# A four-layer graph network: TensorE's outputs and the residual rows by tile in the first node stage, and the combining first in the first node layer

## The chip, the cores and the metric

The kernel runs on one core of one Trainium2 chip. The time is the device time of one execution in microseconds (us), and the median of several runs is compared. Before the change it is 8783.5 us (3 runs, 8773.5 to 8791.46).

## What is computed

50,000 nodes with 160 features each (64 scalars and 32 vectors of three parts) pass four graph layers. Each layer gathers and weighs messages along 50,000 edges sorted by their target, sums them by node, combines the sums with the node's own row, adds the row of before and normalises. The two places that the change touches are the node half of layer 0 and the node half of layer 1:

```python
# layer 0, the node half; a0 = node_attr
x = node_input + _merge(ps, pv)
s2, v2 = _eq_ln(x, ln2_w0, ln2_b0, ln2_w1)
fs, fv = _eq_lin(s2, v2, f1_ws, f1_bs, f1_wv)
fs = fs * a0
fv = fv * a0[:, :, None]
sc = silu(fs[:, :M0])
fv = fv * sigmoid(fs[:, M0:])[:, :, None]
os_, ov = _eq_lin(sc, fv, f2_ws, f2_bs, f2_wv)   # 64 scalars, 32 vectors
os_ = os_ * a0
ov = ov * a0[:, :, None]
return x + _merge(os_, ov)
# around every layer
x = _layernorm(x + layer(x, ...), axis=-1)
# layer 1, the node half
return sc + alpha * conv
```

All is float32.

## The kernel before

A chunk is 512 nodes: 4 tiles (TILES) of 128, one node to a partition. There are 98 chunks. The work is a row of stages, and each stage goes over all chunks before the next begins: set-up, `node_pre`, `edge_logits`, `edge_softmax`, a join, `node_first` (the first node stage, layer 0), then for layers 1 to 3 `edge_layer`, a join and `node_layer`.

In a stage every engine has its own program, written out in order by `pipeline(engine, chunks, stages)`: in round i each listed step runs for chunk i minus its offset, in the order of the list. Four rounds are the body of a hardware loop; the first and last rounds are written out. The engines meet by semaphores alone: a step waits until a counter shows that another engine's step for some chunk is done. So the order on one engine is fixed, and a step that waits holds up all behind it.

`node_first`, in the order of one round i:

- TensorE (PE): `turn_last` (i-5, transposes of the normalised rows), `turn_norm` (i-2, transposes of `scaled`), `outputs` (i-3), `hidden` (i-2), `turn_sums` (i), `mix_last` (i-5, the rows for the next layer's gather), `project` (i).
- ScalarE (ACT): `copy_out` (i-5), `final_norm` (i-4), `copy_norm` (i-2), `gates` (i-2), `copy_sums` (i), `rows_out` (i-5).
- VectorE (DVE): `activate` (i-3), `final_bias` (i-4), `scale` (i-2), `residual` (i-1), `divide` (i), `combine` (i-3).
- GpSimd (POOL): gathers of the summed messages (i), and the two roots.
- SyncE (SP): loads and stores.

`project`, `outputs` and `mix_last` write the same PSUM columns (two banks from column 1024 on). In `outputs` the bias comes first as one product of the identity with 256 columns, then four products of 64 columns add the scalars on it, then six of 64 columns write the vectors; PSUM holds the 256 scalars of the 4 tiles, then the 384 vector columns by part. VectorE's `combine` takes, for each tile, one operation for the scalars and one for the vectors, multiplies by the node's attribute and adds `base`, which `residual` has written in the same order (L1832). `final_sums` ends with a copy of 8 columns, the row's tail (L712).

`node_layer(1)`, in the order of one round i: VectorE `before` (i; here one operation on 128x4, L884, which needs the gathered sums), `final_bias` (i-2), `combine` (i-1). GpSimd: four gathers for chunk i (L671), then the root of chunk i-2 (L720). TensorE: `front` (i), `turn_out` (i-3), `back` (i), `mix_out` (i-3). ScalarE: `front`, `copy_out` (i-3), `final_norm` (i-2), `rows_out` (i-3). SyncE loads the indices and rows of chunk i once `before` of chunk i-2 is done. Layer 2 has the same lists with a longer `before`; layer 3 has `combine` first.

Of the kernel before, what the change touches and what calls it, by code (L numbers as in the profile page):

```python
# [22 lines left out]
ALU = mybir.AluOpType  # L23
# [3 lines left out]
P = 128  # L27
CHUNK = 512
TILES = CHUNK // P
C0, C1 = 64, 32  # L30
# [121 lines left out]
def gnn_kernel(nc, inp, out):  # L152
# [9 lines left out]
    def two(name, shape, dt=F32, own=None):  # L162
        return [sb(f"{name}_{k}", shape, dt, own) for k in range(2)]
# [16 lines left out]
    with ctx:  # L180
# [589 lines left out]
        def node_layer(layer):  # L770
# [13 lines left out]
            with nc.Block() as block:  # L784
# [88 lines left out]
                def _(dve):  # L873
# [97 lines left out]

                    if with_e:
                        pipeline(dve, chunks, [(before, 0), (lambda s: final_bias(dve, s), 2), (combine, 1)])
                    else:
                        pipeline(dve, chunks, [(combine, 1), (lambda s: final_bias(dve, s), 2), (before, 0)])
# [664 lines left out]
        def node_first():  # L1640
            den_steps, x1_steps, scale_steps, hidden_steps = 10, 2 * TILES + 8, 7, 1
            sum_steps = 2 * TILES + 2 * TILES + 2
            m_at, q_at, v_at, r_at, c_at, b_at, n_at = 48, 56, 60, 68, 76, 84, 88
            SCA, VEC, HID_S, HID_V, GATE = 1024, 1024 + XS, 2048, 2560, 3584
            with ExitStack() as own, nc.Block() as block:
                shares, scaled = two("shares", [P, XD], own=own), two("scaled", [P, XD], own=own)
                squares, base = two("squares_1", [P, XD - XS], own=own), [sb(f"base_{k}", [P, XW], own=own) for k in range(4)]
                first = two("first", [P, XD], own=own)
# [15 lines left out]
                def _(pe):  # L1664
# [20 lines left out]
                    def project(s):  # L1685
                        read = sum_step.after((s.g - 2) * sum_steps - (sum_steps - 2 * TILES))
                        precompute(pe, ets_sb.after(s.g - 4), read)
# [13 lines left out]
                    def mix_last(s):  # L1701
                        read = sum_step.after(ahead(s.g, 3, chunks) * sum_steps - (sum_steps - 2 * TILES))
# [26 lines left out]
                    def outputs(s):  # L1729
                        read = mid_step.after(ahead(s.g, 3, chunks) * x1_steps - (x1_steps - 2))  # L1730
                        precompute(pe, read, ets_sb.after(s.g - 2))
                        pe.wait_ge(ready.sem, 1)
                        pe.wait_ge(ets_sb.sem, ets_sb.after(s.g - 2))
                        pe.wait_ge(gate_sb.sem, gate_sb.after(s.g + 1))
                        pe.wait_ge(hidden_step.sem, hidden_step.after((s.g + 1) * hidden_steps))
                        pe.wait_ge(mid_step.sem, read)
                        pe.matmul(flat[:, SCA:SCA + XS], ident, W("f2_b"), start=True, stop=False)
                        for t in range(TILES):
                            pe.matmul(flat[:, SCA + t * C0:SCA + (t + 1) * C0], hid_s[:, t * P:(t + 1) * P], W("f2_s"),
                                      start=False, stop=(t == TILES - 1))  # L1740
                        for i in range(3):
                            for k in range(2):
                                to = flat[:, VEC + i * P:VEC + (i + 1) * P].rearrange("p (h k c) -> p h k c", h=2, k=2)
                                last = pe.matmul(to[:, :, k, :], hid_v[:, (2 * i + k) * P:(2 * i + k + 1) * P], W("f2_v"),
                                                 start=True, stop=True)
                        last.then_inc(post_mm.sem, 1)
# [4 lines left out]
                @block.scalar  # L1751
                def _(act):
                    def copy_norm(s):
                        act.wait_ge(xt2_mm.sem, xt2_mm.after(s.g + 1))
# [8 lines left out]
                    def gates(s):  # L1763
# [6 lines left out]
                    pipeline(act, chunks, [  # L1770
                        (lambda s: copy_out(act, s, TURN), 5), (lambda s: final_norm(act, s), 4), (copy_norm, 2),
                        (gates, 2), (copy_sums, 0), (lambda s: rows_out(act, s, SCA), 5)])

                @block.gpsimd
                def _(pool):
                    pipeline(pool, chunks, [
                        (lambda s: gather_sums(pool, s, 0, mid_step, x1_steps), 0),
                        (lambda s: root(pool, s, v_at, 2 * TILES, mid_step, x1_steps, root_sb), 2),
                        (lambda s: root(pool, s, 32, TILES, sum_step, sum_steps, root2_sb, 1), 4)])

                @block.vector
                def _(dve):
# [30 lines left out]
                    def residual(s):  # L1813
# [5 lines left out]
                        dve.wait_ge(sum_step.sem, sum_step.after((s.g - 2) * sum_steps))  # L1819
                        dve.wait_ge(scale_step.sem, scale_step.after((s.g - 1) * scale_steps))  # L1820
                        dve.wait_ge(pre_step.sem, pre_step.after((s.g + 1) * den_steps))
                        k = chain.did(dve.tensor_tensor(x1[:, 0:XS], flat[:, SCA:SCA + XS], x[:, 0:XS], ALU.add).then_inc(chain.sem, 1))
                        k = chain.did(dve.tensor_tensor(x1[:, XS:], flat[:, VEC:VEC + XD - XS], x[:, XS:XD], ALU.add).then_inc(chain.sem, 1))
                        chain.did(dve.tensor_copy(b[:, XD:], x[:, XD:]).then_inc(chain.sem, 1))
                        dve.wait_ge(chain.sem, chain.after(k))
# [5 lines left out]
                            ALU.add).then_inc(chain.sem, 1))  # L1831
                        chain.did(dve.tensor_tensor(b[:, 0:XD], x1[:], x[:, 0:XD], ALU.add).then_inc(chain.sem, 1))  # L1832
                        dve.wait_ge(chain.sem, chain.after(c))
# [6 lines left out]
                    def scale(s):  # L1840

                        chain = Chain(scale_step, s.g, scale_steps)
                        dve.wait_ge(chain.sem, chain.after(0))
                        st, x1, to, attrs = stats[s.quad], first[s.slot], scaled[s.slot], base[s.quad][:, XD:XD + TILES]
                        dve.wait_ge(root_sb.sem, root_sb.after(s.g + 1))
# [30 lines left out]
                    def combine(s):  # L1876
# [367 lines left out]
```

## Time and profile before

| | |
|---|---|
| median of 3 runs | 8783.5 us |
| profiled execution | 8718.24 us, span 8716.4 us |
| TensorE busy | 6567.3 us (75%) |
| VectorE busy | 6227.6 us (71%) |
| ScalarE, GpSimd busy | 4108.6 us (47%), 5093.1 us (58%) |
| granted TensorE clock, mean | 0.853 |
| `node_first` | from about 2600 to 3980 us of the span |
| node half of layer 1 | from about 4785 to 5480 us of the span |

The shares are means over ten stages with different limits. What counts for the change is which wait ends last within one round of the two stages. The clock is given as a part of 2.4 GHz; its lower level is 0.5.

### The profile page before, as it was taken

How to read it: one execution, taken by the hardware profiler on the slowest of the kernel's cores; microseconds unless marked ns; L12 is line 12 of the kernel's file. 1: busy time of each engine (PE TensorE's matmuls, PEld its weight loads, DVE VectorE, ACT ScalarE, POOL GpSimd, SP SyncE). 2: the span in 40 equal slices, each digit the busy share in tenths (PEclk: the TensorE clock that was granted, in tenths of full speed). 3: DMA queues.
4: the chain of work that ended last, by engine and by line, in shares of the span. 5: the costliest groups of instructions: out<-in, count | busy, mean ns of one | idle time of the engine just before them, and what ended most of it. 6: DMA issues, size and time to landing. Idle time of an engine off the chain costs nothing. (4 is left out here: it accounts for less than half of the span.)

```text
span 8716.4 us, 182003 instructions
## 1 busy us (share of the span) xinstructions
PE 6567.3 (75%) x41992; PEld 5838.5 (67%) x41992; DVE 6227.6 (71%) x20668; ACT 4108.6 (47%) x9608; POOL 5093.1 (58%) x4620
## 2 busy tenths in 40 slices
PE   3667777774557888888998666899865679999555
PEld 3455666664447777777888666788755569998554
DVE  4667888885548888885665667566588877775787
ACT  1334555552224444444444667444366654444444
POOL 4668888884435444444554777555466644443777
PEclk9887888885559999999999888899978889999665
DMA  6872333337873333333444566445455544443555
GB/s 133 182 173 79 89 89 88 90 85 145 164 155 92 99 96 99 99 98 102 125 126 114 181 190 192 120 123 125 110 169 166 170 129 120 119 120 106 154 162 155
DMA packets 910393, 1118.45 MB, mean 128 GB/s; under 512 B 458518, under 2 KB 546422, under 8 KB 910032
## 3 DMA queue, kind: packets, MB, share of 16 engines
q1 hardware_dynamic: 728032, 812.69, 33.4%
q0 software_dynamic: 182144, 303.64, 14.7%
q14 instruction: 175, 1.43, 0.1%
q8 instruction: 42, 0.69, 0.0%
HBM read 650.35 MB, written 465.65 MB: 128 GB/s over the span
## 5 line engine op out<-in xcount | busy, mean ns | idle before, releaser
L451 POOL DMA_INDIRECT erow<-e_rows,edge_idx x1176 | 1247.3, 1061 | 1229.6 <-issue 1137.3
L671 POOL DMA_INDIRECT agg<-seg_rows,edge_idx x1568 | 1554.3, 991 | 656.4 <-issue 483.2
L720 POOL TENSOR_TENSOR stats<-stats,power 128x8 f32<-128x8 f32 (+1 forms) x588 | 751.8, 1279 | 866.1 <-DVE xo L712 444.4
L400 PE MATMUL banks<-w_all,xt 128*128 128x128 f32 (+1 forms) x2352 | 546.2, 369 | 795.7 <-DVE y_more L945 259.5
L400 PEld LDWEIGHTS banks<-w_all,xt 128*128 128x128 f32 x2352 | 429.3, 248 | 879.8 <-issue 872.2
L486 PEld LDWEIGHTS banks<-seg,mid 128*128 128x128 f32 x7840 | 931.9, 194 | 15.1
L486 PE MATMUL banks<-seg,mid 128*128 128x128 f32 x7840 | 933.4, 277 | 0.0
L534 ACT ACTIVATE mid_t<-banks 128x512 f32<-128x512 f32 x980 | 585.1, 597 | 315.3 <-PE banks L486 311.7
L403 PE MATMUL banks<-w_all,xt 128*128 128x128 f32 x3528 | 657.7, 339 | 0.0
L403 PEld LDWEIGHTS banks<-w_all,xt 128*128 128x128 f32 x3528 | 617.5, 254 | 0.0
L498 PE MATMUL banks<-w_all,mid_t 128*128 128x161 f32 (+1 forms) x2352 | 583.9, 330 | 2.8 <-ACT res L539 2.8
L539 ACT ACTIVATE res<-banks 128x644 f32<-128x644 f32 (+1 forms) x294 | 218.0, 742 | 687.4 <-PE banks L505 685.5
L1207 POOL DMA_INDIRECT work<-src_table,edge_idx x392 | 456.0, 1163 | 108.2 <-issue 108.2
L608 POOL DMA_INDIRECT row_of_dram<-where_back x196 | 255.4, 1303 | 363.1 <-DMA where_back<-place_dram 315.8
L1207 POOL DMA_INDIRECT y<-dst_table,edge_idx x392 | 387.5, 989 | 119.5 <-issue 119.2
L474 PE MATMUL banks<-w_all,hid_p 128*128 128x384 f32 (+1 forms) x1176 | 454.8, 509 | 3.2 <-ACT hid_p L516 3.2
L738 ACT ACTIVATE xo<-y,stats 128x64 f32<-128x64 f32 (+1 forms) x1200 | 428.8, 443 | 45.7 <-DVE stats L727 45.7
L498 PEld LDWEIGHTS banks<-w_all,mid_t 128*128 128x128 f32 x2352 | 378.9, 192 | 89.2 <-issue 38.4
L738 ACT ACTIVATE xo<-y_more,stats 128x64 f32<-128x64 f32 (+1 forms) x1152 | 411.4, 443 | 38.6 <-DVE stats L727 38.5
L505 PE MATMUL banks<-w_all,mid_t 128*128 128x64 f32 x2352 | 423.7, 262 | 0.0
L500 PE MATMUL banks<-w_all,mid_t 128*128 128x96 f32 x2352 | 421.2, 260 | 0.0
L337 DVE TENSOR_TENSOR seg<-dst_row,edge_idx 128x512 f32<-128x512 int32 x294 | 203.1, 691 | 281.9 <-PE banks L486 244.4
(276 smaller groups left out, 18225.2 us busy)
## 6 DMA issues: line engine op xcount, KB each, us to landing
x_rows<-xo SPq DMA_DIRECT2D x294, 324.0 KB, 2.6
xin<-x_rows SPq DMA_DIRECT2D x294, 324.0 KB
e_rows<-ets SPq DMA_DIRECT2D x294, 322.0 KB
dst_row<-in_dst_flat SPq DMA_DIRECT2D x294, 256.0 KB
xin<-in_x SPq DMA_DIRECT2D x196, 324.0 KB, 7.1
seg_rows<-res SPq DMA_DIRECT2D x196, 322.0 KB, 2.6
seg_rows<-res SPq DMA_DIRECT2D x98, 384.0 KB, 2.3
seg_rows<-res SPq DMA_DIRECT2D x98, 338.0 KB, 6.6
```

What stands on the lines that cost most here:

```text
L400: pe.matmul(flat[:, to + k * cols:to + (k + 1) * cols], of[:, k * P:(k + 1) * P], W(w_s), start=True, stop=True)
L403: last = pe.matmul(flat[:, to + 2 * cols + k * P:to + 2 * cols + (k + 1) * P], of[:, (2 + k) * P:(3 + k) * P], W(w_v), start=True, stop=True)
L451: pool.indirect_dma_start(erow[s.quad][:, t, 0:EROW], None, table, bass.IndirectOffsetOnAxis(idx[s.slot][:, t:t + 1], 0),).then_inc(rows_i ...
L474: last = pe.matmul(psum[:, 2 + k, 0:2 * w_cols], hid_p[:, k * P:(k + 1) * P], W(f"fc2_{layer}"), start=True, stop=True)
L486: last = pe.matmul(psum[:, SEG[k], t * P:(t + 1) * P], mid[s.slot][:, t, k * P:(k + 1) * P], seg[s.slot][:, t, :], start=True, stop=True)
L498: pe.matmul(post[:, t, 0:v_at + 96], mid_t[s.slot][:, 0, cut], W(f"pa{layer}"), start=True, stop=False)
L505: last = pe.matmul(post[:, t, v_at + 32:v_at + 96], mid_t[s.slot][:, 2, cut], W(f"pc{layer}"), start=False, stop=True)
L534: act.activation(mid_t[s.slot][:, k, :], bank(SEG[k]), ACT.Copy).then_inc(agg_sb.sem, 1)
L671: pool.indirect_dma_start(agg[s.quad][:, t, 0:SUM_COLS[layer]], None, seg_rows[layer], bass.IndirectOffsetOnAxis(idx[s.slot][:, t:t + 1], ...
L720: pool.tensor_tensor(st[:, at + n:at + 2 * n], st[:, at:at + n], power[:, 0:n], ALU.pow) \
L738: last = act.activation(to, of if at == 0 else of.rearrange("p (i c) -> p i c", i=3), ACT.Identity, bias=st[:, 40 + t:41 + t], scale=st[:, ...
L1207: pool.indirect_dma_start(to[s.slot][:, t, :], None, table, bass.IndirectOffsetOnAxis(idx[s.slot][:, first + t:first + t + 1], 0),).then_i ...
```

## The change

In `node_first`:

- `outputs` writes one run of 160 columns for each tile (64 scalars, then the vectors), two tiles to a PSUM bank. The bias is no longer one product of 256 columns but one of 64 columns for each tile, right ahead of the product that adds on it. 14 products to a chunk where there were 11 (each is two weight loads and two matmuls in the trace).
- `residual` writes `base` in rows of 160 columns for each tile: one operation for the scalars, one for the vectors, instead of one for all; it has one more wait, for a normalisation three chunks back, since ScalarE now reads `base`.
- `combine` has one operation of 160 columns for each tile instead of two.
- The tail of the row is copied by ScalarE, ahead of `final_norm`.

In `node_layer(1)` VectorE runs `combine` (i-1), `final_bias` (i-2), `before` (i).

```diff
-                    if with_e:
+                    if layer == 2:
                         pipeline(dve, chunks, [(before, 0), (lambda s: final_bias(dve, s), 2), (combine, 1)])
                     else:
                         pipeline(dve, chunks, [(combine, 1), (lambda s: final_bias(dve, s), 2), (before, 0)])
...
+            row_at = (0, 512, D, 512 + D)
...
-                        pe.matmul(flat[:, SCA:SCA + XS], ident, W("f2_b"), start=True, stop=False)
                         for t in range(TILES):
-                            pe.matmul(flat[:, SCA + t * C0:SCA + (t + 1) * C0], hid_s[:, t * P:(t + 1) * P], W("f2_s"),
-                                      start=False, stop=(t == TILES - 1))
+                            to = flat[:, SCA + row_at[t]:SCA + row_at[t] + C0]
+                            pe.matmul(to, ident, W("f2_b", cols=(0, C0)), start=True, stop=False)
+                            pe.matmul(to, hid_s[:, t * P:(t + 1) * P], W("f2_s"), start=False, stop=True)
...
+                    def norm(s):
+                        act.wait_ge(sum_step.sem, sum_step.after((s.g + 1) * sum_steps))
+                        act.wait_ge(node_out[s.quad].sem, node_out[s.quad].after(s.quarter))
+                        act.activation(xo[s.quad][:, XD:], base[s.quad][:, TILES * D:], ACT.Copy)
+                        final_norm(act, s)
...
+                        dve.wait_ge(norm_sb.sem, norm_sb.after(s.g - 3))
...
-                        chain.did(dve.tensor_tensor(b[:, 0:XD], x1[:], x[:, 0:XD], ALU.add).then_inc(chain.sem, 1))
+                        rows = by_tile(b[:, 0:TILES * D])
+                        chain.did(dve.tensor_tensor(rows[:, :, 0:C0], by_tile(x1[:, 0:XS]), by_tile(x[:, 0:XS]), ALU.add).then_inc(chain.sem, 1))
+                        chain.did(dve.tensor_tensor(rows[:, :, C0:].rearrange("p t (i c) -> p i t c", i=3), by_part(x1[:, XS:]),
+                                                    by_part(x[:, XS:XD]), ALU.add).then_inc(chain.sem, 1))
...
-                            a = b[:, XD + t:XD + t + 1]
-                            chain.did(dve.scalar_tensor_tensor(
-                                yy[:, t, 0:C0], by_tile(flat[:, SCA:SCA + XS])[:, t, :], a, by_tile(b[:, 0:XS])[:, t, :],
+                            a = b[:, TILES * D + t:TILES * D + t + 1]
+                            k = chain.did(dve.scalar_tensor_tensor(
+                                yy[:, t, :], flat[:, SCA + row_at[t]:SCA + row_at[t] + D], a, b[:, t * D:(t + 1) * D],
                                 ALU.mult, ALU.add).then_inc(chain.sem, 1))
-                            k = chain.did(dve.scalar_tensor_tensor(
-                                yy[:, t, C0:].rearrange("p (i c) -> p i c", i=3), by_part(flat[:, VEC:VEC + 3 * P])[:, :, t, :],
-                                a, by_part(b[:, XS:XD])[:, :, t, :], ALU.mult, ALU.add).then_inc(chain.sem, 1))
                         dve.wait_ge(chain.sem, chain.after(k))
-                        final_sums(dve, s, chain, b[:, XD:])
+                        final_sums(dve, s, chain, None)
```

TensorE in the body of `node_first`'s loop, before, from `project` over `turn_norm` and `outputs` to `hidden` (`banks` is PSUM, `w_all` the weights with the identity, `hid_s` and `hid_v` the hidden rows):

```order
466 L1692 MATMUL banks<-w_all 128x256
467 L1694 MATMUL banks<-w_all,xt 128x128 x2
468 L1697 MATMUL banks<-w_all,xt 128x128 x3
469 L394 MATMUL banks<-w_all,scaled 128x128 x5
470 L1737 MATMUL banks<-w_all 128x256
471 L1739 MATMUL banks<-w_all,hid_s 128x64 x4
472 L1744 MATMUL banks<-w_all,hid_v 128x2x32 x6
473 L1715 MATMUL banks<-xt,w_all 128x128 x4
```

The same place now:

```order
474 L1698 MATMUL banks<-w_all,xt 128x128 x3
475 L394 MATMUL banks<-w_all,scaled 128x128 x5
476 L1740 MATMUL banks<-w_all 128x64
477 L1741 MATMUL banks<-w_all,hid_s 128x64
478 L1740 MATMUL banks<-w_all 128x64
479 L1741 MATMUL banks<-w_all,hid_s 128x64
480 L1740 MATMUL banks<-w_all 128x64
481 L1741 MATMUL banks<-w_all,hid_s 128x64
482 L1740 MATMUL banks<-w_all 128x64
483 L1741 MATMUL banks<-w_all,hid_s 128x64
484 L1746 MATMUL banks<-w_all,hid_v 128x2x32 x6
485 L1716 MATMUL banks<-xt,w_all 128x128 x4
```

One wide product and four narrow ones have become eight narrow ones; nothing else moved on TensorE.

VectorE in the node half of layer 1, one round before (`agg` holds the gathered sums, `y` and `y_more` the rows of this chunk and the next):

```order
1668 L884 TENSOR_TENSOR stats<-agg,xin 128x4
1669 L726 REGISTER_ALU
1670 L727 SCALAR_TENSOR_TENSOR stats<-stats 128x4
1671 L930 REGISTER_ALU
1672 L932 REGISTER_ALU
1673 L943 TENSOR_TENSOR y<-banks,xin 128x4x64
1674 L945 TENSOR_TENSOR y<-banks,xin 128x3x4x32
```

And now, the end of one round and the head of the next:

```order
1645 L708 TENSOR_SCALAR stats<-stats 128x4
1646 L710 ISA
1647 L712 COPY xo<-xin 128x8
1648 L726 REGISTER_ALU
1649 L727 SCALAR_TENSOR_TENSOR stats<-stats 128x4
1650 L884 TENSOR_TENSOR stats<-agg,xin 128x4
1651 L138 REGISTER_ALU
1652 L138 COMPARE_AND_BRANCH
1653 L943 TENSOR_TENSOR y_more<-banks,xin 128x4x64
```

L884, which waits for gathered rows, stood ahead of the combining of the chunk before it (L943 to L712) and now stands behind it.

## Rows read from the trace of the kernel before

**Rows 1.** Busy time by stretch: `node_first`'s loop; columns in the first line.
```profile
core 0: us, PE busy (x) PEld busy (x) DVE busy (x) ACT busy (x) POOL busy (x), PEclk, DMA share, GB/s
2709.40:3909.00 1199.60, 997.45 (x7570) 947.54 (x7569) 1007.96 (x4620) 554.46 (x1392) 582.16 (x523) 0.94 0.33 98
```
**Rows 2.** Waits in `node_first` (2700 to 3900 us); columns in the first line.
```profile
engine line waited for: us in total, times, longest us
DVE hid_v L1871 <- issue: 68.0, 22, 3.3
...
PE banks L394 <- ACT xt L759: 57.5, 65, 0.9
PE banks L394 <- DVE scaled L1861: 45.9, 22, 2.3
```
**Rows 3.** Timeline of TensorE: each round's start of `project`; columns in the first line.
```profile
start us, us, engine line op out<-in xcount [idle before <-releaser]
3300.49 0.67 PE L1692 MATMUL banks<-w_all 128*128 128x256 f32 x2 [1.04 <-ACT ets L766]
3313.12 0.67 PE L1692 MATMUL banks<-w_all 128*128 128x256 f32 x2 [1.13 <-ACT ets L766]
3330.55 0.67 PE L1692 MATMUL banks<-w_all 128*128 128x256 f32 x2 [1.14 <-ACT ets L766]
...
3425.11 0.67 PE L1692 MATMUL banks<-w_all 128*128 128x256 f32 x2 [1.13 <-ACT ets L766]
3439.11 0.67 PE L1692 MATMUL banks<-w_all 128*128 128x256 f32 x2 [1.14 <-ACT ets L766]
```
**Rows 4.** Timeline of VectorE over the end of a loop body in `node_first`.
```profile
3302.66 0.42 DVE L1822 TENSOR_TENSOR first<-banks,xin 128x256 f32<-128x256 f32 x1 [0.44 <-PE banks L1697]
...
3311.53 0.17 DVE L712 COPY xo<-base 128x8 f32<-128x8 f32 x1
3314.88 0.95 DVE L1871 SCALAR_TENSOR_TENSOR hid_v<-tanh_g,banks 128x768 f32<-128x768 f32 x1 [3.18 <-issue]
...
3317.10 0.42 DVE L1861 TENSOR_TENSOR scaled<-scaled,stats 128x256 f32<-128x256 f32 x1
```
**Rows 5.** Timeline: TensorE's weight loads (PEld) and matmuls, one ScalarE row, `outputs` to `hidden`.
```profile
3304.17 0.30 PEld L1737 LDWEIGHTS banks<-w_all 128*128 128x128 f32 x2
3305.49 1.42 PEld L1744 LDWEIGHTS banks<-w_all,hid_v 128*128 128x128 f32 x12
3306.21 0.68 ACT L1756 ACTIVATE xt<-banks 128x640 f32<-128x640 f32 x1
3309.17 0.97 PEld L1725 LDWEIGHTS banks<-xt,w_all 128*128 128x128 f32 x8
3309.28 1.06 PE L1725 MATMUL banks<-xt,w_all 128*128 128x128 f32 x8
```
**Rows 6.** Timeline of VectorE in `node_first`: base rows, a 384-column operation, `combine`.
```profile
3305.47 0.81 DVE L1832 TENSOR_TENSOR base<-first,xin 128x640 f32<-128x640 f32 x1
3308.25 0.27 DVE L1884 SCALAR_TENSOR_TENSOR y<-banks,base 128x64 f32<-128x64 f32 x1
3310.03 1.01 DVE L692 BATCH_NORM_STATS2 stats<-y 128x6 f32<-128x160 f32 x4
...
3316.63 0.55 DVE L1858 TENSOR_TENSOR scaled<-first,stats 128x384 f32<-128x384 f32 x1
```
**Rows 7.** Timeline of VectorE in the node half of layer 1, one round.
```profile
5106.90 0.16 DVE L884 TENSOR_TENSOR stats<-agg,xin 128x4 f32<-128x4 f32 x1 [1.56 <-DMA agg<-seg_rows,edge_idx]
5109.02 1.27 DVE L953 SCALAR_TENSOR_TENSOR y<-agg,stats,y 128x160 f32<-128x160 f32 x4
5110.34 1.00 DVE L692 BATCH_NORM_STATS2 stats<-y 128x6 f32<-128x160 f32 x4
...
5111.84 0.17 DVE L712 COPY xo<-xin 128x8 f32<-128x8 f32 x1
```
**Rows 8.** Groups by line, layer 1's node half, 4900 to 5400 us.
```profile
line engine op names shapes xcount | busy us, mean ns | idle before us <-releasers
L671 POOL DMA_INDIRECT agg<-seg_rows,edge_idx x285 | 286.0, 1003 | 85.5 <-issue 85.2 <-DVE xo L712 0.3
L720 POOL TENSOR_TENSOR stats<-stats,power 128x4 f32<-128x4 f32 x72 | 74.7, 1038 | 54.6 <-DVE xo L712 52.9 <-DMA edge_idx<-row_of_dram 1.3
L884 DVE TENSOR_TENSOR stats<-agg,xin 128x4 f32<-128x4 f32 x72 | 11.9, 165 | 131.6 <-DMA agg<-seg_rows,edge_idx 130.3 <-DVE xo L712 1.3
```
**Rows 9.** The instructions of line L884: count, durations, first and last start.
```profile
L884 DVE TENSOR_TENSOR stats<-agg,xin x98: 161/164/225, 4792.8 to 5467.7; 128x4 f32<-128x4 f32 x98
```

More of the change, by code:

```diff
@@ L1640, in node_first @@
         def node_first():
-            den_steps, x1_steps, scale_steps, hidden_steps = 10, 2 * TILES + 8, 7, 1
-            sum_steps = 2 * TILES + 2 * TILES + 2
+            den_steps, x1_steps, scale_steps, hidden_steps = 10, 2 * TILES + 9, 7, 1
+            sum_steps = TILES + 2 * TILES + 1
+            row_at = (0, 512, D, 512 + D)
             m_at, q_at, v_at, r_at, c_at, b_at, n_at = 48, 56, 60, 68, 76, 84, 88
@@ L1646, in node_first @@
                 shares, scaled = two("shares", [P, XD], own=own), two("scaled", [P, XD], own=own)
-                squares, base = two("squares_1", [P, XD - XS], own=own), [sb(f"base_{k}", [P, XW], own=own) for k in range(4)]
+                squares, base = two("squares_1", [P, XD - XS], own=own), [sb(f"base_{k}", [P, TILES * D + 2 * TILES], own=own) for k in range(4)]
                 first = two("first", [P, XD], own=own)
@@ L1685, in project @@
                     def project(s):
-                        read = sum_step.after((s.g - 2) * sum_steps - (sum_steps - 2 * TILES))
+                        read = sum_step.after((s.g - 2) * sum_steps - (sum_steps - TILES))
                         precompute(pe, ets_sb.after(s.g - 4), read)
@@ L1701, in mix_last @@
                     def mix_last(s):
-                        read = sum_step.after(ahead(s.g, 3, chunks) * sum_steps - (sum_steps - 2 * TILES))
+                        read = sum_step.after(ahead(s.g, 3, chunks) * sum_steps - (sum_steps - TILES))
                         precompute(pe, read)
@@ L1736, in outputs @@
                         pe.wait_ge(mid_step.sem, read)
-                        pe.matmul(flat[:, SCA:SCA + XS], ident, W("f2_b"), start=True, stop=False)
                         for t in range(TILES):
-                            pe.matmul(flat[:, SCA + t * C0:SCA + (t + 1) * C0], hid_s[:, t * P:(t + 1) * P], W("f2_s"),
-                                      start=False, stop=(t == TILES - 1))
+                            to = flat[:, SCA + row_at[t]:SCA + row_at[t] + C0]
+                            pe.matmul(to, ident, W("f2_b", cols=(0, C0)), start=True, stop=False)
+                            pe.matmul(to, hid_s[:, t * P:(t + 1) * P], W("f2_s"), start=False, stop=True)
                         for i in range(3):
                             for k in range(2):
-                                to = flat[:, VEC + i * P:VEC + (i + 1) * P].rearrange("p (h k c) -> p h k c", h=2, k=2)
-                                last = pe.matmul(to[:, :, k, :], hid_v[:, (2 * i + k) * P:(2 * i + k + 1) * P], W("f2_v"),
+                                at, step = SCA + row_at[k] + C0 + i * C1, row_at[2 + k] - row_at[k]
+                                to = flat[:, at:at + 2 * step].rearrange("p (h c) -> p h c", h=2)[:, :, 0:C1]
+                                last = pe.matmul(to, hid_v[:, (2 * i + k) * P:(2 * i + k + 1) * P], W("f2_v"),
                                                  start=True, stop=True)
@@ L1770, in _ @@
                     pipeline(act, chunks, [
-                        (lambda s: copy_out(act, s, TURN), 5), (lambda s: final_norm(act, s), 4), (copy_norm, 2),
+                        (lambda s: copy_out(act, s, TURN), 5), (norm, 4), (copy_norm, 2),
                         (gates, 2), (copy_sums, 0), (lambda s: rows_out(act, s, SCA), 5)])
@@ L1778, in _ @@
                         (lambda s: root(pool, s, v_at, 2 * TILES, mid_step, x1_steps, root_sb), 2),
-                        (lambda s: root(pool, s, 32, TILES, sum_step, sum_steps, root2_sb, 1), 4)])
+                        (lambda s: root(pool, s, 32, TILES, sum_step, sum_steps, root2_sb), 4)])
                 @block.vector
@@ L1823, in residual @@
                         k = chain.did(dve.tensor_tensor(x1[:, XS:], flat[:, VEC:VEC + XD - XS], x[:, XS:XD], ALU.add).then_inc(chain.sem, 1))
-                        chain.did(dve.tensor_copy(b[:, XD:], x[:, XD:]).then_inc(chain.sem, 1))
+                        chain.did(dve.tensor_copy(b[:, TILES * D:], x[:, XD:]).then_inc(chain.sem, 1))
                         dve.wait_ge(chain.sem, chain.after(k))
@@ L1843, in scale @@
                         dve.wait_ge(chain.sem, chain.after(0))
-                        st, x1, to, attrs = stats[s.quad], first[s.slot], scaled[s.slot], base[s.quad][:, XD:XD + TILES]
+                        st, x1, to, attrs = stats[s.quad], first[s.slot], scaled[s.slot], base[s.quad][:, TILES * D:TILES * D + TILES]
                         dve.wait_ge(root_sb.sem, root_sb.after(s.g + 1))
```

## The prediction, made before the result was known

> **What bounds the kernel now.** I read the busy time by stretch first, to see which stages the change touches, then the waits of each of the two stages, then one round of each in the timeline. The sums are made against the profiled execution, 8718.24 us (span 8716.4); the median of the runs is 8783.5 us, 65 us or 0.75% more. I take the change in microseconds over unscaled, since 1% of it is about 1 us.
>
> In `node_first` TensorE and VectorE are each busy 83 to 84% of 1199.6 us [rows 1]. There are 87 rounds in 1200 us (65 and 22 waits before the transposes of `scaled`, L394, [rows 2]), so 13.79 us a round. The timeline shows that this mean is of two kinds [rows 3]. An ordinary round is 12.63 us (3300.49 to 3313.12). There TensorE decides: it stands still only for ScalarE's copies (1.13 us before `project`, and 57.5 / 65 = 0.88 us before the transposes of `scaled` [rows 2]), and VectorE waits for it (0.44 us before L1822 [rows 4]). Every fourth round is 14.0 us (3425.11 to 3439.11) or 17.43 us (3313.12 to 3330.55). At that place the loop's body ends on VectorE, and L1871 comes 3.18 us after the instruction before it, with "issue" as the reason [rows 4]; 22 such stalls add to 68.0 us, and TensorE's transposes of `scaled` then wait 45.9 us in 22 times, 2.09 us each, for VectorE's L1861 [rows 2]. The rest of the long rounds is the clock: its mean is 0.94 over 1199.6 us [rows 1]. With levels 1 and 0.5 it was at the lower one for 12%, 144 us, in which a busy TensorE loses half, 72 us. The sum closes: four rounds at 13.79 are 55.2, four at 12.63 are 50.5, so 4.7 us a loop, 22 loops, 103 us; 22 times 1.4 us (14.0 less 12.6) is 31, and 72 the clock.
>
> In the node half of layer 1 the round is (5467.7 - 4792.8) / 97 = 6.96 us [rows 9]. GpSimd waits for L712, the end of VectorE's combining, 52.9 us in 72 rounds, and VectorE's L884 waits for gathered rows, 130.3 us [rows 8]. Each waits for the other. From L884 at 5106.90 to the end of L712 at 5112.01 are 5.1 us [rows 7]; the root is 1.04, four gathers with their gaps (286.0 + 85.5) / 285 x 4 = 5.2 [rows 8]; what remains of two rounds (13.9) is some 2.5 us until the rows have landed. It is a ring of 13.9 us that spans two rounds.
>
> **The change part by part, `node_first`.**
>
> TensorE. 16 weight loads instead of 10 stand ahead of the vector products. Eight loads take 0.97 us and twelve 1.42 [rows 5], so 0.112 us each: 16 x 0.112 = 1.79. Before, from the first load of L1737 to that of L1744 it was 3305.49 - 3304.17 = 1.32. So +0.47. But `hidden` starts only when ScalarE's copy L1756 ends at 3306.89, while TensorE's loads of L1744 are through at 3305.49 + 12 x 0.112 = 3306.83 and the next starts some 0.1 later, at 3306.94. That 0.1 us is cover, so the net is +0.34 to +0.47; I take 0.34, in 98 chunks +33 us. It is on the path, since TensorE sets the ordinary round. Bounds: +0.2 and +0.47, 20 to 46 us.
>
> What this measures against is the cost by columns. The loads are full 128x128 ones whatever the columns that follow [rows 5], and the spacing was 0.112 us with 128 columns too. The Trainium skill, "TensorE: Matmul & The Clock Gate", section "Back-to-back issue gap", gives the isolated spacing as N/2.4 + 2.5 ns, by which 256 + 4 x 64 columns and 8 x 64 would cost the same and this term would be near nothing (8640 us in all); its next section has a load at P/1.2, 107 ns for 128 columns, and with this the trace agrees.
>
> VectorE. `combine`: eight operations take from 3308.25 to 3310.03, 1.78 us, until the statistics [rows 6]; four of 160 columns in layer 1 from 5109.02 to 5110.34, 1.32 us [rows 7]. There they read SBUF and here PSUM, as the eight do. -0.46. The tail's copy goes: -0.17 [rows 4]. `base`: 0.81 us become 0.42 + 0.55 in length [rows 4, 6], +0.16 at most; starts overlap, I take +0.08. Together -0.55 (bounds -0.4 to -0.65). In an ordinary round it is worth nothing, since TensorE decides. The new wait for a normalisation three chunks back has behind it all of `residual`, `divide` and `combine`, and through them TensorE's `project`; ScalarE did that normalisation a whole round earlier, so 0.
>
> ScalarE. One copy of 8 columns, 0.1 to 0.2 us, ahead of eight normalising operations, then L1756. It ends at some 3307.05 instead of 3306.89; TensorE now comes to it at 3307.3. Hidden. Its two waits (combining of the round before, store of eight chunks ago) are over by then.
>
> The end of the loop's body. The stall itself should stay: VectorE's body is still far longer than in any other stage. But VectorE reaches it 0.55 us earlier, and TensorE needs the result 0.34 us later. The transposes of `scaled` wait 2.09 us now, 1.2 more than in an ordinary round; of that 1.2 - 0.55 - 0.34 = 0.3 is left. So the long round loses 1.1 of its 1.4 us: 22 x 1.1 = -24 us. And TensorE is then idle some 1.2 us there where it was 2.09, nearest to the ordinary round's 0.9, in which the clock never falls. I take the whole 72 us back. Bounds: 0 and -72.
>
> The Trainium skill, "Runtime: NRT & Kernel Launch", section "Instruction fetch mechanics", says a taken branch to a target outside the two pages of the instruction memory forces a fetch. It would explain why this loop, the longest, stalls; no row here shows pages. By it the stall could also vanish, which in the sum is worth 7 us more.
>
> `node_first`: +33 - 24 - 72 = -63 us (bounds +22 and -76).
>
> **The node half of layer 1.** The combining of chunk i-1 no longer stands behind L884 of chunk i. It now needs only its own sums and runs while the gathers of chunk i are still under way. The ring then spans three rounds instead of two, 13.9 / 3 = 4.6 us a round, and no longer decides. What is late next is GpSimd itself: its round without the wait for L712 is (500 - 52.9) / 72 = 6.21 us, against 6.94 now [rows 8]. All of it would be 0.73 x 98 = 72 us. VectorE has 5.1 us of work in 6.2, so L884 may come late now and then, and through it the load of the indices two chunks on (SyncE starts it when L884 is done), and TensorE's `back` must be ready one round sooner. I take two thirds, 0.5 us a round, -49 us; bounds 0 (or +20, if L884 is what is late) and -72.
>
> **Sum.** -63 - 49 = -112 us: 8606 us against the profiled execution, 8672 us against the median.
>
> **The rivals.**
>
> B. The clock still falls after the stall. For it: only the length of the gap changes and the stall is the same 3 us; if the gap stays near 1.6 us half of the falls may remain. Against: the gap works out nearer 0.9. Then `node_first` is +33 - 24 = +9 and the time 8783.5 + 9 - 49 = 8744 us.
>
> C. Layer 1 gains nothing: a new wait takes the place of the old one. Combining right after L884 needs `back` of the same chunk, which needs the row load of that chunk, which SyncE issues only after L884 of two chunks before; or the gathers slow down as they come closer. For it: the DMA queues are busiest in this stage. Against: GpSimd waits for L712 by name. 8783.5 - 63 = 8721 us. B and C together: 8793 us, no change.
>
> D. Slower: in `outputs` each bias product now stands directly ahead of the product that adds to the same columns. If the second waits until the first is in PSUM, a pass costs its length, 1.06 - 7 x 0.112 = 0.275 us [rows 5], instead of 0.112: 16 x 0.275 = 4.4 us for 1.32, +3.1 us x 98 = +302, with no gain of the clock -24 and -49 beside it: about 9010 us. It decides once the narrow products cost 1.5 us a chunk more than before, 0.18 us a pass. Against: each product's own two passes add to the same columns and follow at 0.112 already.
>
> E. The program is shorter, and another stage's loop comes to lie so that it stalls 3 us each time: 22 x 3 = 66 us beside the forecast, 8738 us. No other loop shows such a stall, and their bodies are shorter.
>
> **Chances.** Forecast 0.60, with its own range 8640 to 8710 (layer 1 between a third and all of its 72, TensorE's term between its ends, part of the clock). B 0.13, C 0.15, both together 0.05, D 0.05, E 0.02. A measurement of this kernel can tell about 0.2%, 18 us, from no change. Faster: 0.60 + 0.13 + 0.15, less a little for B's and C's poor ends, 0.86. Same 0.07, slower 0.07. The range for 8 in 10 is 8630 to 8755: it holds the forecast, C and the better B.
>
> **What would show it.** Right: ordinary rounds of `project` 12.9 to 13.0 us apart; long rounds 13.3; the mean clock of the stage near 1.0; the first operation of `activate` still 3 us late at the loop's end; the wait of the `scaled` transposes about 1.2 us there. In layer 1 a round of 6.3 to 6.5 us, GpSimd's wait for L712 gone. Wrong: a clock still at 0.94, a stage round over 13.8, a layer 1 round of 6.9 with GpSimd or VectorE waiting for index or row loads, or narrow products further apart than 0.112 us.

## The result and the profile after

The kernel after takes 8628.56 us in the median (8622.57 to 8638.99); the kernel before, timed beside it, 8779.48 us (8773.5 to 8791.46). The ratio is 0.9828, 95% interval 0.9811 to 0.9845: 151 us less, give or take 15. The forecast was 8672 us, 112 less, and its range ended at 8630. Direction and places were right; the time fell 1.4 us outside the range, which is far less than the interval of 15, and, as the runs below show, most of the gain of `node_first` came in another way than forecast.

The profiled execution of after took 8625.71 us (span 8623.9) at a mean clock of 0.863.

The view of busy time by stretch, for the kernel after; the first stretch answers to [rows 1] (columns: length, busy time of each engine with its instructions, clock, DMA share, GB/s):

```profile
2709.40:3909.00 1199.60, 1014.45 (x8587) 975.36 (x8587) 1013.17 (x4528) 597.24 (x1569) 613.94 (x550) 1.00 0.36 103
```

The clock is 1.00 where it was 0.94: its lower level is gone from the stage. TensorE is about as busy as before (1014.45 us, it was 997.45) and does 8587 matmuls in the stretch instead of 7570. The waits in `node_first` of after (line waited for, total us, times, longest us), against [rows 2]:

```profile
DVE first L1831 <- PE banks L1698: 116.8, 90, 1.4
...
PE banks L1693 <- ACT ets L766: 101.0, 91, 1.1
PE banks L394 <- ACT xt L759: 83.1, 92, 1.0
DVE hid_v L1883 <- ACT hid_s L1776: 49.0, 92, 1.1
```

Two rows of before have no counterpart: `hid_v` no longer waits with the reason "issue" (68.0 us in 22 times), and the transposes of `scaled` no longer wait for VectorE (45.9 us). They wait for ScalarE's `xt` 92 times, 0.90 us each, in every round alike. The end of a loop body on VectorE's timeline (start, length, in brackets the idle time ahead), against [rows 4]:

```profile
3365.40 0.17 DVE L708 TENSOR_SCALAR stats<-stats 128x4 f32<-128x4 f32 x1
3366.08 0.95 DVE L1883 SCALAR_TENSOR_TENSOR hid_v<-tanh_g,banks 128x768 f32<-128x768 f32 x1 [0.51 <-ACT hid_s L1776]
...
3368.42 0.42 DVE L1873 TENSOR_TENSOR scaled<-scaled,stats 128x256 f32<-128x256 f32 x1
```

The body ends between L708 and L1883. VectorE is idle for 0.51 us there and waits for ScalarE; before it was idle for 3.18 us. The 3 us stall, which the prediction said would stay, is not there. TensorE's rounds, against [rows 3]:

```profile
3315.90 0.67 PE L1693 MATMUL banks<-w_all 128*128 128x256 f32 x2 [1.13 <-ACT ets L766]
3329.01 0.67 PE L1693 MATMUL banks<-w_all 128*128 128x256 f32 x2 [1.14 <-ACT ets L766]
3342.02 0.67 PE L1693 MATMUL banks<-w_all 128*128 128x256 f32 x2 [1.13 <-ACT ets L766]
3354.93 0.67 PE L1693 MATMUL banks<-w_all 128*128 128x256 f32 x2 [1.04 <-ACT ets L766]
3367.93 0.67 PE L1693 MATMUL banks<-w_all 128*128 128x256 f32 x2 [1.13 <-ACT ets L766]
```

The starts are 13.11, 13.01, 12.91 and 13.00 us apart: no long round. Four rounds are 52.0 us, as against 55.2.

The node half of layer 1 of after, its groups by line (busy us, mean ns; idle us ahead of them and what ended it), against [rows 8], and the instructions of L884, against [rows 9]:

```profile
L671 POOL DMA_INDIRECT agg<-seg_rows,edge_idx x318 | 316.4, 995 | 95.2 <-issue 81.5 <-DVE xo L712 11.0 <-DVE y L943 0.6
L720 POOL TENSOR_TENSOR stats<-stats,power 128x4 f32<-128x4 f32 x79 | 87.0, 1101 | 1.9
...
L884 DVE TENSOR_TENSOR stats<-agg,xin x98: 161/164/229, 4763.1 to 5370.9; 128x4 f32<-128x4 f32 x98
```

GpSimd's root L720, which was held 52.9 us by VectorE's L712, has 1.9 us of idle time ahead of it in a stretch of the same length (4800 to 5300 us). What is left of GpSimd's waiting for L712 is 11.0 us ahead of the gathers, in 79 rounds. The round is (5370.9 - 4763.1) / 97 = 6.27 us; it was 6.96.

Stage lengths, between the moves with which VectorE sets up its loops: `node_first` 1361.0 to 1293.2 us (-67.8), node half of layer 1 705.2 to 639.5 (-65.7). That is 133.5 of the 151 us. The edge half of layer 1 is 5.8 shorter, of unchanged code; the stages ahead of `node_first`, unchanged too, came out 38 us longer in this one execution, so single traces can't settle the other 17.

### The profile page after: what moved, and what is told of

Same layout as the page of the kernel before. It is cut to its first block and busy times, and to the rows that moved or that the text cites. A ratio compares the mean times of both kernels' runs of the same rounds, so it can differ in the third digit from the quotient of the medians.

```text
span 8623.9 us, 182979 instructions
## 1 busy us (share of the span) xinstructions
PE 6524.1 (76%) x42580; PEld 5791.9 (67%) x42580; DVE 6173.8 (72%) x20276; ACT 4113.7 (48%) x9706; POOL 5083.8 (59%) x4620
## 3 DMA queue, kind: packets, MB, share of 16 engines
q0 software_dynamic: 182144, 303.64, 15.7%
## 5 line engine op out<-in xcount | busy, mean ns | idle before, releaser
L720 POOL TENSOR_TENSOR stats<-stats,power 128x8 f32<-128x8 f32 (+1 forms) x588 | 757.6, 1289 | 730.9 <-DVE stats L708 306.2
L400 PEld LDWEIGHTS banks<-w_all,xt 128*128 128x128 f32 x2352 | 422.3, 243 | 725.6 <-issue 713.0
L403 PEld LDWEIGHTS banks<-w_all,xt 128*128 128x128 f32 x3528 | 603.8, 248 | 0.0
```

The costliest lines, as they stand in the source:

```text
L400: pe.matmul(flat[:, to + k * cols:to + (k + 1) * cols], of[:, k * P:(k + 1) * P], W(w_s), start=True, stop=True)
L403: last = pe.matmul(flat[:, to + 2 * cols + k * P:to + 2 * cols + (k + 1) * P], of[:, (2 + k) * P:(3 + k) * P], W(w_v), start=True, stop=True)
L720: pool.tensor_tensor(st[:, at + n:at + 2 * n], st[:, at:at + n], power[:, 0:n], ALU.pow) \
```

## The experiments

Theory 1 is that of the prediction: each part works alone, and they add. Its rival was that the stall went because of where the loop's body lies among VectorE's instructions (Theory A below), and not with the length of the body or with what VectorE waits for there (Theory B). The runs stand in four batches, each on a chip of its own and beside the kernel before: e1 to e4 (before 8728.53 us), e5 to e8 (8721.82), e9 to e12 (8972.27, one run) and e13 to e16 (9022.71, one run). e6 and e9 to e16 are single runs; of e9 to e16 only the stall, the falls of the clock and the length of the loop are read.

**e1: the order of layer 1 alone**, in the kernel before:

```diff
-                    if with_e:
+                    if layer == 2:
```

> Only the order on VectorE in the node half of layer 1 is changed (combining, bias, before); node_first is that of the kernel before. Theory 1 (the ring of 13.9 us over two rounds is cut and GpSimd alone sets the round): the node half of layer 1 takes 6.2 us a round, 65 to 70 us less in all, and the kernel is 65 to 70 us faster than before. Rival (the two changes help each other, since 151 us were measured and the two terms taken from the traces are only some 135): 80 us or more. Rival (the layer-1 part was mis-sized low because of something else in that stretch): under 50 us.

8661.71 us, ratio 0.9920 (0.9906 to 0.9933): -67 us. L884 runs from 4810.0 to 5418.2, 6.27 us a round. The stall of `node_first` stays. This is the layer 1 term by itself, and rival C is out.

**e2: `node_first`'s part alone** (the kernel after with `if with_e:` put back):

> Only node_first is changed; layer 1 keeps the old order on VectorE. Theory 1 (the stall of 3 us at the end of VectorE's loop body is gone, and with it the fall of the clock; TensorE's round is 0.4 us longer): 68 us faster than before, rounds of 13.0 us, granted clock 1.00 in the loop. Rival (parts add up to more than the traces' 135): this one gives 85 us or more.

8656.7 us, ratio 0.9913 (0.9897 to 0.9929): -72 us. No stall, clock 1.00, L884 again at 7.01 us a round. The parts add to -139.

**e3: the kernel before, moved.** Ahead of `node_first`'s program on VectorE:

```diff
+                    for k in range(150):
+                        dve.memset(spare[:, k:k + 1], 0.0)
```

> The kernel before with 150 tiny VectorE operations (128x1 memsets into a spare tile) ahead of node_first's VectorE program; nothing in any round is changed, and the memsets cost some 10 us once. Theory A (the stall at the end of the loop body depends on where the body lies in the program, in blocks of instructions): the stall is gone with the body as long as it was, rounds of 12.6 us, clock 1.00, and node_first is about 100 us shorter, 85 to 95 us net. Theory B (the stall comes with the length of the body, 399 instructions against 378, or with what VectorE waits for there): the stall of 3.1 us stays, the rounds stay at 13.8, and the kernel is 0 to 10 us slower than before.

8725.43 us, ratio 0.9997 (0.9987 to 1.0007); the stall stays (68.4 us in 22 times). At this place nothing changed, as by Theory B.

**e4: the kernel after, moved** by 30 memsets in the same way:

> The changed kernel with 30 tiny VectorE operations ahead of node_first's VectorE program. Theory A (place of the body): the stall of 3 us comes back although the body has only 378 instructions. Then it shows what the prediction's own step was worth: with the stall kept, the wait of the transposes of scaled should be about 1.2 us at the loop's end instead of 2.1, the long round 13.3 us, the clock near 1.00, and the time only some 7 us above the changed kernel's. If instead the clock falls again, node_first goes to 14 us a round and the time is 80 us or more above. Theory B (length or waits): no stall, the time of the changed kernel plus 2 us.

8651.25 us, ratio to before 0.9914 (0.9899 to 0.9929), and the stall is back with all of the change's arithmetic in place. Waits, stretch and TensorE's timeline of e4:

```profile
DVE hid_v L1887 <- issue: 77.8, 22, 3.8
...
PE banks L394 <- ACT xt L759: 57.5, 65, 0.9
...
PE banks L394 <- DVE scaled L1877: 36.3, 22, 2.0
```

```profile
2709.40:3909.00 1199.60, 1007.16 (x8072) 965.83 (x8073) 954.38 (x4254) 561.54 (x1475) 582.04 (x521) 0.96 0.34 98
```

```profile
3314.48 0.67 PE L1694 MATMUL banks<-w_all 128*128 128x256 f32 x2 [1.05 <-ACT ets L766]
3327.48 0.67 PE L1694 MATMUL banks<-w_all 128*128 128x256 f32 x2 [1.13 <-ACT ets L766]
3346.80 0.67 PE L1694 MATMUL banks<-w_all 128*128 128x256 f32 x2 [1.14 <-ACT ets L766]
3359.80 0.67 PE L1694 MATMUL banks<-w_all 128*128 128x256 f32 x2 [1.13 <-ACT ets L766]
```

This comes near the case that the prediction worked out: the stall stays, VectorE is sooner, TensorE later. The transposes of `scaled` wait 36.3 / 22 = 1.65 us instead of 2.09. But the long rounds are still long (19.32 us here), and the clock falls after 13 of the 22 stalls, where it fell after 18; each fall is one round of over 16 us. The loop, from the end of its first body to that of its last, is 1215.3 us long, as before (1212.3); in the kernel after it is 1144.6. With the stall the change to `node_first` is worth nothing: 30 memsets ahead of the loop, 1 us of work, make the loop 71 us longer. The timed runs agree: 0.9914 is next to e1's 0.9920, which has none of `node_first`'s change. The same body stalls at one place and not at another, so the place counts, and Theory B is out as the whole answer.

**e5: the kernel before with 95 memsets**, a place at which a body of 399 would lie in two blocks of 256, if a memset took two places:

> The kernel before with 95 memsets of one column ahead of node_first's VectorE program (about 3 us of work, once). Theory A (where the loop's body lies in VectorE's instructions decides whether it stalls; a body of 378 stalls when it begins 30 later, one of 399 when it begins 0 or 150 later; if the body must not lie over three stretches of 256 and a memset takes two places, it is free of the stall when it begins 61 to 118 memsets later, so 95 is near the middle): no stall at the loop's end, every round of project 12.64 us, the clock 1.0 in the stage, node_first about 103 us shorter, 8728 - 103 + 3 = 8628 us or 0.988. Rival (a body of 399 instructions is too long wherever it lies, or a memset takes one place): stall, clock and time as before, 0.9995 to 1.0005.

8725.59 us, ratio 1.000 (0.999 to 1.001), and the stall is there:

```profile
DVE hid_v L1875 <- issue: 66.8, 22, 3.2
...
PE banks L394 <- DVE scaled L1865: 44.6, 22, 2.2
```

The expectation by Theory A was wrong: in its rule, not in the idea, as e9 to e15 show. This run bears on e4 too. TensorE waits 44.6 / 22 = 2.03 us here, about as long as in the kernel before, and yet the clock falls only 14 times (14 rounds of over 16 us), nearly as seldom as in e4.

**e6: the narrow products alone**, in the kernel before:

```diff
-    pe.matmul(flat[:, SCA:SCA + XS], ident, W("f2_b"), start=True, stop=False)
     for t in range(TILES):
-        pe.matmul(flat[:, SCA + t * C0:SCA + (t + 1) * C0], hid_s[:, t * P:(t + 1) * P], W("f2_s"),
-                  start=False, stop=(t == TILES - 1))
+        to = flat[:, SCA + t * C0:SCA + (t + 1) * C0]
+        pe.matmul(to, ident, W("f2_b", cols=(0, C0)), start=True, stop=False)
+        pe.matmul(to, hid_s[:, t * P:(t + 1) * P], W("f2_s"), start=False, stop=True)
```

> The kernel before with the bias of the gated outputs added by four products of 64 columns, each directly ahead of the product that adds to the same columns, instead of one product of 256 columns; everything else as before. The prediction's term: six more weight passes of 0.112 us, so ordinary rounds of project 12.64 + 0.34 to 0.47 = 12.98 to 13.11 us. Rival by columns (a product costs its columns, the weight load is hidden): 12.64. Rival D (the second product waits for the first): 15.7. The stall at the loop's end stays, and with it the falls of the clock: about 22 rounds of 14 to 19 us.

8743.79 us in one run. Weight loads of one round of e6, then two starts of `project`:

```profile
3299.88 0.30 PEld L1739 LDWEIGHTS banks<-w_all 128*128 128x128 f32 x2
...
3301.44 0.30 PEld L1740 LDWEIGHTS banks<-w_all,hid_s 128*128 128x128 f32 x2
3301.67 1.42 PEld L1744 LDWEIGHTS banks<-w_all,hid_v 128*128 128x128 f32 x12
```

```profile
3309.20 0.67 PE L1692 MATMUL banks<-w_all 128*128 128x256 f32 x2 [1.13 <-ACT ets L766]
3322.11 0.67 PE L1692 MATMUL banks<-w_all 128*128 128x256 f32 x2 [1.05 <-ACT ets L766]
```

Sixteen loads in 3301.67 - 3299.88 = 1.79 us, 0.112 each, as worked out; the ordinary rounds are 12.99 us in the median where before had 12.64. A pass of 64 columns costs its weight load, and not its columns. (The ten loads of before took 1.32 us and not 1.12, so this does not hold for its product of 256 columns.) Rival D (each narrow product waiting for the one before) is out, it wanted 15.7 us.

**e7: two bias products instead of four**, in the kernel after, each over two tiles of one bank:

```diff
-    for t in range(TILES):
-        to = flat[:, SCA + row_at[t]:SCA + row_at[t] + C0]
-        pe.matmul(to, ident, W("f2_b", cols=(0, C0)), start=True, stop=False)
-        pe.matmul(to, hid_s[:, t * P:(t + 1) * P], W("f2_s"), start=False, stop=True)
+    for k in range(2):
+        step = row_at[2 + k] - row_at[k]
+        to = flat[:, SCA + row_at[k]:SCA + row_at[k] + 2 * step].rearrange("p (h c) -> p h c", h=2)[:, :, 0:C0]
+        pe.matmul(to, ident, W("f2_b", cols=(0, 2 * C0)), start=True, stop=False)
+        for t in (k, 2 + k):
+            pe.matmul(flat[:, SCA + row_at[t]:SCA + row_at[t] + C0], hid_s[:, t * P:(t + 1) * P], W("f2_s"),
+                      start=False, stop=(t >= 2))
```

> The kernel after with the bias of two tiles of one bank added by one product of 128 columns (two bias products instead of four, four weight passes fewer). If each pass costs 0.112 us on the path, the round of project is 13.00 - 0.45 = 12.6 us, less what ScalarE's copy then makes TensorE wait: 12.65 to 12.8 us, 20 to 35 us less in 98 rounds, about 0.997 of the kernel after. If the passes are hidden: 13.0. VectorE's program is the same, so no stall at the loop's end.

8560.94 us (8553.95 to 8566.19), ratio to before 0.9813 (0.9798 to 0.9827); the mean round is 12.74 us, and there is no stall. It is the fastest version here: its slowest run is below the fastest of the kernel after on the same chip (8568.0). `project` in e7:

```profile
3338.03 0.67 PE L1693 MATMUL banks<-w_all 128*128 128x256 f32 x2 [1.13 <-ACT ets L766]
3350.86 0.67 PE L1693 MATMUL banks<-w_all 128*128 128x256 f32 x2 [1.14 <-ACT ets L766]
3363.60 0.67 PE L1693 MATMUL banks<-w_all 128*128 128x256 f32 x2 [1.13 <-ACT ets L766]
```

Its four spared passes would be 0.45 us; 0.26 came. In the kernel before, `outputs` took the same 1.3 us and the round was 12.64; where the last 0.1 us is was not tried.

**e8: the kernel after again**, on the chip of e5 to e7:

> The kernel after as it is, on the chip on which its parts are run again. If the two parts only add (0.9920 and 0.9913): 0.9834, about 8583 us where the kernel before takes 8728. If they help each other: 0.982 or less. Rounds in node_first 13.00 us, in the node half of layer 1 6.3 us.

8575.77 us (8568.0 to 8596.45), ratio 0.9833 (0.9815 to 0.9850), 146 us less. The sum of the parts, 139 by e1 and e2 on their chip, is inside that interval (131 to 161): they add, and no help of one to the other needs to be assumed.

**e9 to e16: where the stall comes from.** The kernel after with 64, 128, 224, 256, 8, 376 and 384 memsets ahead, and, in e16, with five in each `residual`, which is 20 in a body and also 15 in the first rounds, written out ahead of the loop:

> The kernel after with 64 memsets of one column ahead of node_first's VectorE program. Where does a body of 378 instructions stall? It doesn't at 0, and does at 30. Model M (it must lie within two neighbouring stretches of 256): stall, node_first's VectorE loop 1215 us. Model N (a store of some 384 instructions, filled in stretches of 64 or fewer): no stall, 1145 us.

> The same with 128 memsets. Model M: at the edge, either may be. Model N: no stall, 1145 us.

> The same with 224 memsets. Model M: no stall, 1145 us. Model N in stretches of 64: stall, 1215 us; in stretches of 32 or fewer: no stall.

> The same with 256 memsets. Both models: as at 0, no stall, 1145 us. If it stalls, the place of the body does not repeat with 256 instructions, and the rule stays open.

> The kernel after with 8 memsets of one column ahead of node_first's VectorE program. Model Q (the body must lie within three neighbouring stretches of 128 instructions, 384 in all, so one of 378 fits at 7 places of 128): 8 is outside wherever the 7 places begin: stall of about 3 us at the loop's end. Looser rules that fit the runs so far (free of it from 0 up to 29): no stall.

> The same with 376 memsets, 8 short of three times 128. Model Q: outside, stall. Looser rules (free of it a little below a multiple of 128): no stall.

> The same with 384 memsets, three times 128. Model Q: as at 0, no stall.

> The kernel after with five memsets of one column added in each turn's residual, 20 in a body, which makes it 398 long; they take some 0.03 us each. Model Q: longer than 384, so a stall wherever it lies, as in the kernel before. Rival (only the place counts, not the length): no stall.

All that was seen of the stall, by the body's length in VectorE's instructions and the instructions put ahead. On the chips of e9 to e16 the loop is some 35 to 50 us longer even without the stall, and the clock falls there without it: 8 times in e10, 4 in e12, 8 in e15. So compare those loops with each other. The stall costs less there: with it at every turn, e9's clock falls 8 times too, and its loop is 25 us longer than that of e10 and 40 us longer than that of e12.

| body | put ahead | kernel | stall | `hid_v` waits, "issue" | loop |
|---|---|---|---|---|---|
| 399 | 0 | before | yes | 68.0 us, 22 times | 1212.3 us |
| 399 | 95 | e5 | yes | 66.8, 22 | 1198.8 |
| 399 | 150 | e3 | yes | 68.4, 22 | 1215.8 |
| 378 | 0 | after | no | none | 1144.6 |
| 378 | 8 | e13 | yes | 95.1, 23 | 1278.8 |
| 378 | 30 | e4 | yes | 77.8, 22 | 1215.3 |
| 378 | 64 | e9 | yes | 80.7, 23 | 1218.9 |
| 378 | 128 | e10 | no | 4.1, once | 1194.4 |
| 378 | 224 | e11 | yes | 74.7, 22 | 1233.6 |
| 378 | 256 | e12 | no | 1.7, once | 1178.8 |
| 378 | 376 | e14 | yes | 142.1, 23 | 1353.4 |
| 378 | 384 | e15 | no | 1.7, once | 1190.7 |
| 398 | 15 | e16 | yes | 79.3, 23 | 1232.1 |

The waits of three of them, at 376, 384 and 398:

```profile
DVE hid_v L1887 <- issue: 142.1, 23, 7.0
```

```profile
DVE hid_v L1887 <- issue: 1.7, 1, 1.7
```

```profile
DVE hid_v L1886 <- issue: 79.3, 23, 3.8
```

Models M and N, made for e9 to e12, both failed: M at 224 (stall, where it had none), N in stretches of 64 or fewer at 64 (stall, where it had none). What is left is Model Q: a body free of the stall lies within three neighbouring stretches of 128 instructions, so one of over 384 never is, and one of 378 is at seven places of 128. Its four expectations, put down before e13 to e16, all came true, the one 8 short of a multiple of 128 among them; the looser rules named beside it failed at 8 and at 376.

Two things carry less than they seem to. e16 is no test of the length by itself: its body begins 15 instructions later, between 8 and 30, where a body of 378 stalls too. The length is shown by the kernels before and after: from the last branch of the stage before to the end of the first body VectorE has 590 instructions in the trace of before and 569 in that of after, so both bodies begin 191 instructions on, at the same place, and the one of 399 stalls while the one of 378 does not. And the number 384 is inferred. Free were places a multiple of 128 apart, not free were 8 on either side, and no body between 378 and 398 was run; that one of over 384 stalls at every place was seen at three for 399 and at one for 398. That the instructions are fetched anew there is an inference from this pattern too; no record shows a fetch. Nor was it tried whether the kernel before, at a body of 384 or less, has rounds of 12.64 us throughout.

## Why the prediction was right in its sign and wrong in its steps

**Layer 1: right mechanism, mis-sized term.** "I take two thirds, 0.5 us a round, -49 us." The round went from 6.96 to 6.27 us, 0.69 less: -66 in the trace, -67 in e1, nearly the whole bound of 72. The discount was for VectorE's L884 or the index loads coming late now and then. L884 still waits for gathered rows, 66.0 us in 79 rounds, but behind that wait nothing stands now on which GpSimd's root depends at once. GpSimd sets the round, and its floor of 6.21 was the right number. This is 17 of the 39 us by which the forecast was off.

**TensorE's term: right.** +0.34 us a chunk was said, 13.00 - 12.64 = +0.36 came, and e6 shows it alone (+0.35). The rule of the isolated spacing, N/2.4 + 2.5 ns for N columns (the Trainium skill, "TensorE: Matmul & The Clock Gate", section "Back-to-back issue gap"), would have priced it at nothing. The same section says that this formula counts too little at small N, since it leaves out the weight load, and the trace agrees: by it a product of 64 columns is 29 ns, by an estimate, and e6 shows 112.

**The step that failed: "The stall itself should stay: VectorE's body is still far longer than in any other stage."** It did not stay. The body went from 399 instructions to 378, and at the place where both begin that is short enough: no stall, no long round, no fall of the clock. The prediction held that the length mattered and compared it with the other loops', all much shorter, without asking how much shorter is short enough. It had a rule at hand, that of the Trainium skill, "Runtime: NRT & Kernel Launch", section "Instruction fetch mechanics", with a vanished stall as a possible outcome, and priced that outcome at 7 us more because it had already booked the clock in full. The size of that rule, two pages of 256 instructions, is not what the runs show: it is Model M, and e11 stalls where it has no stall.

**"I take the whole 72 us back" failed with it.** The reason given was that TensorE would be idle about 1.2 us at the stall, near the ordinary 0.9 at which the clock never falls. In e4 it is idle 1.65 us. Of this 0.45 is the growth of the stall itself (77.8 / 22 = 3.54 us, where it was 68.0 / 22 = 3.09), so the arithmetic of 1.2 was sound for a stall that stays as it is. At 1.65 us the clock still fell in 13 of 22, and in e6, at 37.5 / 22 = 1.70 us, in 15; the stage gained nothing. This is rival B, forecast at +9 us for `node_first` and given 0.13; e4's loop is +3 us. A wait of 1.2 us itself was not run. Nor does the length of the wait explain the number of falls: with the unchanged body, at waits of 2.03 to 2.10 us, it fell 18 times in before and in e1, 19 in e3 and 14 in e5. What decides whether a given stall is followed by a fall stays open.

**So -63 against -68 is a right number by a wrong way.** +33 for TensorE came; -24 and -72 for the loop's end and the clock came as one -103, the whole excess of the long rounds which the prediction had itself summed up (22 times 4.7 us): 0.36 x 98 - 103 = -68. Its "7 us more" is the difference. That the new body fits at its place is luck: with 30 instructions more ahead of it (e4) the same change is worth nothing in this stage, and with 8 more (e13, on another chip) it stalls as well.

**Rivals.** C fell with e1, D with e6. E (another loop comes to stall) did not occur: in the kernel after no other loop has a wait of that length with the reason "issue" turn after turn. Of the 39 us, 17 are layer 1's and 5 `node_first`'s. The last 17 have no step: they are about as large as the interval (15 us), and by e1 and e2 the sum is 139, not 151.

**The range.** With layer 1 at its bound of -72 and the stage at -70 the sum was 8641. With both terms as measured, -68 and -66, it is 8649.5, inside the range. So the miss of the range itself is made by what no term explains. The low end of 8630 left 11 us for what separates one execution from the median and one comparison from the next. Two comparisons of the same pair of kernels gave -151 and -146 us.

## What to carry to other kernels

Where a loop's turn costs some 3 us with the reason "issue", count the instructions of the body on that engine and see where it begins, before pricing anything else by it: all that was seen here fits a body that has to lie within three stretches of 128, and fitting it was worth more than all the arithmetic. Make such a body short enough to fit anywhere (by the rule inferred here, 256 or fewer fit at every place; this was not tried), since 8 instructions more ahead of it can bring the stall back. When two engines wait for each other over a ring of rounds, breaking the ring gives back the time down to the floor of the next engine, and a discount on that needs a row of its own.

## What the runs showed of the hardware

- A short loop-end stall can cost more than itself: 22 stalls of 3 us, of which TensorE saw 1.2 us each beyond its ordinary wait, lengthened the stage by 103 us, since the granted clock fell from 2.4 to 1.2 GHz after 18 of them.
- How often the clock falls is not set by the length of TensorE's wait alone: 14 to 19 of 22 at waits of 2.03 to 2.10 us (before, e1, e3, e5), 13 and 15 at 1.65 and 1.70 (e4, e6), none at 0.90 (after). On two other chips it fell 4 to 8 times in the loop without any stall (e10, e12, e15), and 8 times with one at every turn (e9), where the stall cost 25 to 40 us and not 71 to 103.
- Where a loop's body begins decides whether VectorE stalls at its end: one of 378 instructions is free at 0, 128, 256 and 384 instructions more ahead and stalls at 8, 30, 64, 224 and 376.
- The size of the stall depends on the place too: 3.0 (66.8 / 22) to 3.5 us (77.8 / 22) a turn at most places, 4.1 (95.1 / 23) at 8, and 6.2 (142.1 / 23) at 376.
- A float32 product of 64 columns costs its two passes of 0.112 us, the weight load's time, whether it adds to the columns of the product right ahead of it or not (e6: sixteen loads in 1.79 us).
